# A decoder layer on one core: reciprocal denominators written widened by VectorE, the first group's projections in idle banks, and the last two attention rows in two lanes

## The chip, the core and the metric

The kernel runs on one core of one Trainium2 chip. A core has five engines, each with a queue of its own that it works off in order: TensorE (PE; its weight loads are shown apart, as PEld), VectorE (DVE), ScalarE (ACT), GpSimd (POOL) and SyncE (SP), which here only issues DMAs. Engines wait for each other through semaphores. The metric is the device time of one execution in microseconds (us).

## What is computed

64 rows of 128 tokens by 512 features pass through one decoder layer of three parts, each with a layer norm ahead and a residual add behind:

```python
x = x + mixer(layernorm(x))                 # state space mixer
x = x + cross_attention(layernorm(x), ctx)  # banded attention, 8 heads
x = x + experts(layernorm(x))               # top 2 of 8 experts

# mixer
h_in, gate = split(x @ in_proj_w.T)                  # 1024 channels each
u  = silu(causal_conv4(h_in) + conv_b)
ts, Bm, Cm = split(u @ x_proj_w.T)                   # 128, 16, 16
dt = softplus(ts @ dt_proj_w.T + dt_proj_b)
h  = scan(exp(dt * A), dt * u * Bm)                  # 16 states for each channel
y  = ((h * Cm).sum(states) + D * u) * silu(gate)
return y @ out_proj_w.T

# attention of one row (the 512 features are the sequence, the 128 tokens the embedding)
attn = softmax(q @ k.T / 4 within a band of 64)      # 8 heads of 16
o = (attn @ v) @ w_out.T + b_out
return w_ct.T @ (relu(o.T) * ctx) + b_ct
```

## The kernel before

The 64 rows are taken in 32 groups of two (`GB = 2`, `NG = 32`, so `NT = 256` columns). The work is a software pipeline over groups, written out by hand. `iteration(g, cur, nxt, p1, p2)` stands once in each engine's block. It runs the 64 scan steps of group `g` (`cur`), the preparation of group `g + 1` (`nxt`: layer norm, input projections, convolution, `ts`, B and C rows, step sizes), the output projection and attention of group `g - 1` (`p1`), and the experts of group `g - 2` (`p2`). The order on each engine is the order of the lines in `iteration`: there is no scheduler at run time. Iteration -1 only prepares group 0, iterations 1 to 31 have scans and attention both, iteration 32 has only the attention of the last group and the experts of the one before, iteration 33 only the last experts.

The scan of one step takes one decay tile that ScalarE writes into one of two PSUM banks (`decays`), one product that GpSimd writes into a ring of eight SBUF slots (`times_b`), and VectorE's scan instruction (`scan`). The result is multiplied by C, 40 times on GpSimd and 24 times on VectorE (`times_c`), and TensorE sums it over states by transposes into bank 2 (`y_sum`).

PSUM has eight banks: 0 and 1 for decays, 2 for `y_sum`, 3 (`PS_B`) for every projection of the preparation, 4 to 7 (`PS_ATT`) for attention, experts and the output projection.

In the preparation each projection of group `j` goes through the one bank `PS_B`. `h_in(j, q)` makes 256 channels of `h_in`. `tap3` (ScalarE) and six instructions of `conv` (VectorE) read it from the bank, so the next `h_in` or `gate_in` waits for `conv_done`. `gate_raw` copies a gate projection out. `ts_in`, `bc_in_rows` and four `dt_in` follow through the same bank. The weights `w_in` come in eight pieces through two SBUF slots; SyncE issues a piece when the projection that used its slot is done.

Attention of row `b` of a group goes, per row: `proj` (q and k), `v`, four pairs of scores `s` and row maximum `max`, `shift` and `addq`, four `st` (transposed scores) with eight `exp`, two `av` with two copies `o`, then `den` (TensorE transposes the outputs, which carry the softmax sums in every 32nd column), `rden`, `rep`, `on`, `wo`, `enc`, `ct` and `x2`. Rows share one set of tiles (`qk`, `probs`, `xb`, `v_aug`, `nmax`, `o_sb`, `enc`) and the banks 4 to 7, so the two rows of a group follow each other. Around the denominators VectorE takes 32 reciprocals per partition out of PSUM, ScalarE repeats each 32 times, and TensorE transposes the 1024 columns back (`rep`, which waits for `rden_wide`):

```python
nc.vector.reciprocal(rden[:].rearrange("p (j a) -> p j a", j=NJ), ps[:, PS_ATT + 2:PS_ATT + 4, DH:512:32])
nc.scalar.copy(rden_rep.rearrange("p (a r) -> p a r", r=32),
               rden[:].rearrange("p (a r) -> p a r", r=1).to_broadcast([P, NBLK * NHEAD, 32]))
```

Of the kernel before, what the change touches and what calls it, by code (L numbers as in the profile page):

```python
# [5 lines left out]
def decoder_layer(nc, x_d, ctx_d, w_in_d, conv_w_d, conv_b_d, w_xt_d, w_xbc_d, w_dt_d, dt_b_d, a_log_d,  # L6
# [9 lines left out]
    P = 128  # L16
    B, T, H = x_d.shape
    GB = 2
# [29 lines left out]
    with stack:  # L48
# [57 lines left out]
        rden = sb("rden", [P, NBLK * NHEAD])  # L106
# [12 lines left out]
        def part(mem, at, *dims):  # L119
# [45 lines left out]
        den_ps, rden_done, rden_wide, rrep_ps, on_done, wo_ps, enc_used, ct_ps, x2_done = [  # L165
            sem(k) for k in ("den_ps", "rden_done", "rden_wide", "rrep_ps", "on_done", "wo_ps", "enc_used", "ct_ps", "x2_done")]
# [45 lines left out]

        @block.sync
        def _(sp):
# [18 lines left out]
            def context(i):  # L233
                reached(sp, ln_aggr["e"], i)
                sp.dma_start(enc[:], ctx_d[i]).then_inc(enc_in, 16)

            def iteration(g, cur, nxt, p1, p2):
# [6 lines left out]
                if p1:  # L244
                    context((g - 1) * GB)
# [18 lines left out]
                if p1:  # L264
                    context((g - 1) * GB + 1)
# [29 lines left out]
        def _(pool):  # L295
# [36 lines left out]

            def iteration(g, cur, nxt, p1, p2):
                if p1:
                    times_c(g - 1, 62)
                if cur:
                    times_b(g, 0)
                    times_b(g, 1)
                    times_b(g, 2)
                if p2:  # L340
                    rstd("e", g - 2, 0, 2)
                if cur:
                    times_b(g, 3)
# [5 lines left out]
                    times_b(g, 6)  # L349
                    times_b(g, 7)  # L350
                    times_b(g, 8)
                    times_c(g, 5)
                    times_b(g, 9)
                    times_c(g, 6)
                    times_b(g, 10)
                if nxt:
                    rstd("a", g + 1, 0, 2)
                if cur:
                    times_b(g, 11)
                if p1:  # L360
                    rstd("t", g - 1, 0)
                if cur:
                    times_c(g, 8)
                    times_b(g, 12)
                    times_b(g, 13)
                    times_b(g, 14)
                    times_c(g, 10)
                    times_b(g, 15)
                    times_b(g, 16)
                    times_c(g, 11)  # L370
# [3 lines left out]
                    times_b(g, 19)  # L374
                    times_c(g, 14)
                if p1:
                    rstd("t", g - 1, 1)
                if cur:
                    times_b(g, 20)
                    times_c(g, 16)  # L380
                    times_b(g, 21)
                    times_c(g, 18)
                    times_b(g, 22)
                    times_c(g, 19)
# [1568 lines left out]
```

## Time and profile before

| | us |
|---|---|
| median of 3 runs | 4977.84 (4977.36 to 4978.13) |
| the profiled execution, whole | 4972.81 |
| its span in the trace | 4971.0 |
| TensorE busy | 4574.1 (92%) |
| VectorE busy | 4434.0 (89%) |
| ScalarE busy | 4400.9 (89%) |
| GpSimd busy | 4196.7 (84%) |

The span is what the trace covers; 1.8 us of the profiled execution lie around it. The profile page gives the busy time of each engine, the chain of work that ended last, and the costliest groups of instructions; the trace behind it answers by stage, by line and by wait. Most of the span is the same iteration repeated, so one stretch of one period stands for it, and the opening and the end are read apart.

### The profile page before, as it was taken

The numbers are of one execution on the slowest core, as the hardware profiler recorded it, in microseconds if no ns is written. First come the engines' busy times: TensorE is split into PE (matmuls) and PEld (weight loads), VectorE is DVE, ScalarE is ACT, GpSimd is POOL, SyncE is SP. The second block draws the span as 40 slices with busy tenths as digits, with TensorE's granted clock in tenths as the row PEclk, the third lists the DMA queues.
The fourth block names the chain that finished last, engine by engine and source line by source line (L and its number), as shares of the span: only waits on it lengthen the run. The fifth ranks groups of instructions, "written<-read, shape, count | busy, mean of one in ns | idle before, by whom it ended". The sixth has DMA issues, their size and how long they took to land.

```text
span 4971.0 us, 143017 instructions
## 1 busy us (share of the span) xinstructions
PE 4574.1 (92%) x52548; PEld 3357.0 (68%) x52548; DVE 4434.0 (89%) x6051; ACT 4400.9 (89%) x9310; POOL 4196.7 (84%) x3467
## 2 busy tenths in 40 slices
PE   4799999999999999999999999999999999999976
PEld 3666666766766776776776767676666677666653
DVE  2899999999999999999999999999999999999961
ACT  3798999999999999999999999999999999999862
POOL 2988898888898888898888898888889888888860
PEclk8899999999999999999999999999999999999996
DMA  3212222212222221222221222221222221122100
GB/s 124 79 46 71 76 78 78 82 54 67 76 78 78 82 69 52 82 76 78 78 82 38 85 77 75 81 82 40 80 76 78 78 82 56 64 77 77 65 14 7
DMA packets 119316, 350.46 MB, mean 71 GB/s; under 512 B 18688, under 2 KB 19456, under 8 KB 118528
## 3 DMA queue, kind: packets, MB, share of 16 engines
q1 hardware_dynamic: 118656, 341.51, 20.7%
q8 instruction: 432, 7.08, 0.6%
q14 instruction: 228, 1.87, 0.1%
HBM read 323.64 MB, written 17.83 MB: 69 GB/s over the span
## 4 chain that ended last, share of the span: by engine, by line
PE 47%; DVE 18%; POOL 12%; issue 11%; ACT 8%; DMA 2%; DVEq 1%; SPq 0%; ACTq 0%; POOLq 0%
PE ps L1204 9%; PE ps L1156 9%; POOL ring L320 8%; PE ps L1224 5%; DVE ring L1542 5%; POOL ring L329 4%; DVE ps L1542 4%; PE ps L1100 4%; PE ps L1111 3%; DVE nmax L1564 3%; ACT ps L498 3%; PE ps L1072 3%; PE ps L1233 2%; DMA x_new<-in_x 2%; PE ps L1034 1%
## 5 line engine op out<-in xcount | busy, mean ns | idle before, releaser
L320 POOL TENSOR_TENSOR ring<-du,bc 128x512 f32<-128x512 f32 x2048 | 2579.3, 1277 | 486.6 <-PE ps L1156 368.0
L498 ACT ACTIVATE ps<-delta,a_neg 128x254 f32<-128x254 f32 x4096 | 1771.6, 468 | 39.5 <-DVE ring L1542 31.3
L329 POOL TENSOR_TENSOR ring<-ring,bc 128x512 f32<-128x512 f32 x1280 | 1621.6, 1277 | 110.7 <-DVE ring L1542 109.5
L1542 DVE TENSOR_TENSOR_SCAN ring<-ps,ring 128x512 f32<-128x512 f32 x1280 | 1542.5, 1213 | 143.9 <-ACT ps L498 123.9
L1156 PE MATMUL ps<-ident,ring 128*128 128x128 f32 x8192 | 1073.3, 276 | 70.2 <-POOL ring L329 65.5
L1156 PEld LDWEIGHTS ps<-ident,ring 128*128 128x128 f32 x8192 | 925.0, 142 | 179.1 <-issue 99.6
L1542 DVE TENSOR_TENSOR_SCAN ps<-ps,ring 128x512 f32<-128x512 f32 x768 | 933.5, 1215 | 48.8 <-ACT ps L498 39.2
L1526 DVE TENSOR_TENSOR ring<-ps,bc 128x512 f32<-128x512 f32 x768 | 526.4, 685 | 19.0
L657 ACT ACTIVATE probs_mem<-ps 128x768 f32<-128x768 f32 (+1 forms) x512 | 449.8, 912 | 66.8 <-PE ps L1100 63.4
L1224 PE MATMUL ps<-w_in,xt_a 128*128 128x256 f32 x2048 | 484.2, 391 | 20.9 <-ACT delta L550 12.0
L1204 PE MATMUL ps<-xt_a,w_in 128*128 128x256 f32 x2048 | 475.9, 386 | 8.5 <-DVE hc L1646 4.1
L1224 PEld LDWEIGHTS ps<-w_in,xt_a 128*128 128x128 f32 x2048 | 390.2, 194 | 123.8 <-issue 43.0
L1186 PE MATMUL ps<-w_outp,yz 128*128 128x512 f32 x1024 | 465.6, 598 | 8.5 <-ACT yz L591 4.9
L1204 PEld LDWEIGHTS ps<-xt_a,w_in 128*128 128x128 f32 x2048 | 381.5, 191 | 73.7 <-issue 9.9
L1646 DVE SCALAR_TENSOR_TENSOR hc<-ps,conv_w,hc 128x254 f32<-128x254 f32 (+2 forms) x768 | 359.8, 476 | 58.1 <-ACT hc L602 39.9
L1564 DVE TENSOR_REDUCE nmax<-ps 128x8 f32<-128x1280 f32 x256 | 377.7, 1475 | 32.0 <-PE ps L1072 32.0
L1186 PEld LDWEIGHTS ps<-w_outp,yz 128*128 128x128 f32 x1024 | 187.5, 191 | 202.1 <-issue 188.2
L1072 PE MATMUL ps<-qk 32*32 32x160 f32 (+2 forms) x16384 | 296.1, 297 | 0.0
L1100 PE MATMUL ps<-qk 32*128 32x192 f32 (+1 forms) x4096 | 271.9, 380 | 0.0
L1047 PE MATMUL ps<-xb,w_qk 128*128 128x512 f32 x512 | 251.4, 604 | 2.5 <-ACT ps L518 1.1
L1111 PE MATMUL ps<-probs_mem,v_aug 128*32 128x192 f32 (+1 forms) x4096 | 227.8, 364 | 18.6 <-ACT probs_mem L657 18.6
L498 ACT ACT_TABLE_LOAD x187 | 239.9, 1283 | 3.3
(140 smaller groups left out, 6381.0 us busy)
## 6 DMA issues: line engine op xcount, KB each, us to landing
w_in<-in_w_in SPq DMA_DIRECT2D x256, 512.0 KB, 3.6
bc<-bc_rows SPq DMA_DIRECT2D x256, 512.0 KB, 5.5
x_new<-in_x SPq DMA_DIRECT2D x32, 512.0 KB, 6.7
x_res<-in_x SPq DMA_DIRECT2D x32, 512.0 KB, 6.2
enc<-in_ctx SPq DMA_DIRECT2D x64, 256.0 KB, 3.2
out<-x_att SPq DMA_DIRECT2D x32, 512.0 KB, 3.2
w_outp<-in_w_outp SPq DMA_DIRECT2D x1, 2048.0 KB, 7.9
bc_rows<-bc_sb SPq DMA_DIRECT2D x128, 8.0 KB, 1.5
```

The source lines that it names most:

```text
L320: nc.gpsimd.tensor_tensor(ring[:, s % RING, :].rearrange("p (n t) -> p n t", n=2), du[:, q % 2, (ic % 2) * NT:(ic % 2 + 1) * NT].rearrange ...
L329: nc.gpsimd.tensor_tensor(ring[:, s % RING, :], ring[:, s % RING, :], bc[:, s % RS, 2:4, :].rearrange("p a t -> p (a t)"), ALU.mult).then_ ...
L498: nc.scalar.activation(ps[:, bank("step", s), (n % 2) * NT:(n % 2 + 1) * NT].rearrange("p (b t) -> p b t", b=GB)[:, :, 1:T], delta[:, ic, ...
L657: nc.scalar.activation(probs[:, :, blk, lo:hi], ps[:, PS_ATT:PS_ATT + 4, (n % 2) * WIN + lo:(n % 2) * WIN + hi], ACT.Exp).then_inc(p_done, 1)
L1100: last = nc.tensor.matmul(ps[:, PS_ATT + hp, a * WIN + lo:a * WIN + hi], qk[r:r + 32, 2 + j, blk * P:(blk + 1) * P], qk[r:r + 32, j, at:at ...
L1156: last = nc.tensor.matmul(ps[:, PS_Y, b * T:(b + 1) * T], ring[:, t % RING, n * NT + b * T:n * NT + (b + 1) * T], ident[:], start=False, s ...
L1186: last = nc.tensor.matmul(ps[:, PS_ATT + b, :], yz[:, ic, b * T:(b + 1) * T], w_outp[:, ic, :], start=(ic == 0), stop=(ic == NI - 1))
L1204: last = nc.tensor.matmul(ps[:, PS_B, a * NT:(a + 1) * NT], w_in[:, slot, k, a * P:(a + 1) * P], xt_a[:, k, :], start=(k == 0), stop=(k == ...
L1224: last = nc.tensor.matmul(ps[:, PS_B, b * NT:(b + 1) * NT], xt_a[:, k, b * T:(b + 1) * T], w_in[:, slot, k, :], start=(k == 0), stop=(k == ...
L1526: nc.vector.tensor_tensor(ring[:, s % RING, :], ps[:, bank("step", s), :], bc[:, s % RS, 2:4, :].rearrange("p a t -> p (a t)"), ALU.mult). ...
L1542: nc.vector.tensor_tensor_scan(state, ps[:, bank("step", s), :], ring[:, s % RING, :], 0.0, ALU.mult, ALU.add).then_inc(h_done, 1)
L1564: nc.vector.tensor_reduce(nmax[:, n].rearrange("p j (a r) -> p a j r", r=32)[:, :, :, DH], ps[:, PS_ATT:PS_ATT + 4, 0:NJ * NEAR].rearrange ...
```

## The change

Four things change, in one new version.

**Denominators.** `rden` and the semaphore `rden_wide` are gone. VectorE's reciprocal now reads a view of the 32 PSUM columns that repeats each 32 times and writes the 1024 columns of `rden_rep` itself; ScalarE's copy is gone; TensorE's `rep` waits for `rden_done`.

**First group.** `prep_bank(j, use, q)` gives for group 0 (`first(j)`) the banks 4 to 7 to the four `h_in`, 4 to `ts`, 5 to the B and C rows, and 6, 7, 4 to the first three `dt_in`; gates stay in `PS_B`. Their waits for the shared bank go. The order of iteration -1 is written as `first_iteration`: the third gate projection moves ahead of `ts_in`, the first `dt_in` ahead of `bc_in_rows`, and `soft_one` ahead of `soft_ln`.

**Last group.** A second set of tiles, semaphores and banks (0 to 3), a `Lane`, is laid over tiles that are idle once the last scans are over (`hc0`, `bc`, `xt_a`). In iteration 32 row 1 uses it, and the order of that iteration, `last_iteration`, interleaves the two rows. GpSimd clears the new `v_aug` and `nmax` there (`second_lane`).

**Order.** The lines of `iteration` stand in another order on all engines but SyncE; no instruction is added to or taken from the repeated iteration but for the denominators.

```diff
+        def prep_bank(j, use, q=0):
+
+            if not first(j):
+                return PS_B
+            return {"h": PS_ATT + q, "ts": PS_ATT, "bc": PS_ATT + 1, "dt": (PS_ATT + 2, PS_ATT + 3, PS_ATT, PS_B)[q]}[use]
...
+        def lane(g, b):
+
+            return lanes[1 if isinstance(g, int) and g == NG and b == 1 else 0]
...
-                else:
-
-                    act.wait_ge(rden_done, i + 1)
-                    nc.scalar.copy(rden_rep.rearrange("p (a r) -> p a r", r=32),
-                                   rden[:].rearrange("p (a r) -> p a r", r=1).to_broadcast([P, NBLK * NHEAD, 32])).then_inc(rden_wide, 1)
...
-                    pe.wait_ge(rden_wide, i + 1)
+                    pe.wait_ge(L.rden_done, i + 1)
...
-                if q < 2:
+                if first(j):
+                    pass
+                elif q < 2:
...
-                        last = nc.tensor.matmul(ps[:, PS_B, a * NT:(a + 1) * NT], w_in[:, slot, k, a * P:(a + 1) * P],
+                        last = nc.tensor.matmul(ps[:, prep_bank(j, "h", q), a * NT:(a + 1) * NT], w_in[:, slot, k, a * P:(a + 1) * P],
...
-                    dve.wait_ge(den_ps, i + 1)
-                    nc.vector.reciprocal(rden[:].rearrange("p (j a) -> p j a", j=NJ), ps[:, PS_ATT + 2:PS_ATT + 4, DH:512:32]).then_inc(rden_done, 1)
+                    dve.wait_ge(L.den_ps, i + 1)
+                    nc.vector.reciprocal(
+                        L.rden_rep.rearrange("p (j a r) -> p j a r", j=NJ, r=32),
+                        ps[:, L.bank + 2:L.bank + 4, DH:512:32].rearrange("p j (a r) -> p j a r", r=1)
+                        .to_broadcast([P, NJ, NBLK * NHEAD // NJ, 32])).then_inc(L.rden_done, 1)
```

In the order that follows, scans are printed as SCALAR_TENSOR_TENSOR on `ps` or `ring`. On VectorE, at the denominators of row 1 in a repeated iteration, before:

```order
L1542 SCALAR_TENSOR_TENSOR ps<-ps,ring 128x512
L1574 RECIPROCAL rden<-ps 128x32
L1525 REGISTER_ALU
L1526 TENSOR_TENSOR ring<-ps,bc 128x512
L1539 ISA
L1542 SCALAR_TENSOR_TENSOR ring<-ps,ring 128x512
L1532 REGISTER_ALU
L1535 TENSOR_TENSOR yg<-ps,gate_t 128x256
L1578 TENSOR_TENSOR o_sb<-ps,o_sb 128x512 x2
```

At the same place in the changed kernel:

```order
L1773 SCALAR_TENSOR_TENSOR ring<-ps,ring 128x512
L1807 RECIPROCAL probs_mem<-ps 128x1024
L1770 REGISTER_ALU
L1773 SCALAR_TENSOR_TENSOR ring<-ps,ring 128x512
L1814 TENSOR_TENSOR o_sb<-ps,o_sb 128x512 x2
```

The reciprocal writes 1024 columns in place of 32, and one instruction, a scan, stands between it and the use of its result in place of three.

On TensorE, in the last iteration with scans, from `den` of row 1 to `rep` and `wo`, before:

```order
L1121 MATMUL ps<-ident,o_sb 128x128 x8
L1156 MATMUL ps<-ident,ring 128x128 x16
L1130 MATMUL ps<-ident,probs_mem 128x128 x8
L1149 MATMUL ps<-ident,skip 128x128 x2
L1156 MATMUL ps<-ident,ring 128x128 x8
L1136 MATMUL ps<-o_sb,w_o 128x512 x2
```

And in the changed kernel:

```order
L1272 MATMUL ps<-ident,o_sb 128x128 x8
L1307 MATMUL ps<-ident,ring 128x128 x8
L1281 MATMUL ps<-ident,probs_mem 128x128 x8
L1287 MATMUL ps<-o_sb,w_o 128x512 x2
```

Less stands between the transposes that feed the reciprocals and those that take them up.

On TensorE at the very end of attention, in iteration 32, the changed kernel has, from `den` of row 0 on (tiles `hc` and `bc` are row 1's):

```order
L1272 MATMUL ps<-ident,o_sb 128x128 x8
L1262 MATMUL ps<-bc 32x192 x4
L1262 MATMUL ps<-bc 32x256 x8
L1262 MATMUL ps<-bc 32x192 x4
L1281 MATMUL ps<-ident,probs_mem 128x128 x8
L1183 MATMUL ps<-band,ident_bf 32x512 x16
L1251 MATMUL ps<-hc 128x192 x4
L1251 MATMUL ps<-hc 128x256 x4
L1287 MATMUL ps<-o_sb,w_o 128x512 x2
```

Before, nothing of row 1 but two projections stood between row 0's denominators and its end.

## Rows read from the trace of the kernel before

**Rows 1.** The page: span, and busy time of each engine.
```profile
span 4971.0 us, 143017 instructions
PE 4574.1 (92%) x52548; PEld 3357.0 (68%) x52548; DVE 4434.0 (89%) x6051; ACT 4400.9 (89%) x9310; POOL 4196.7 (84%) x3467
```

**Rows 2.** Windows, two periods: stretch, length, busy PE, PEld, DVE, ACT, POOL, clock, DMA.
```profile
1169.00:1316.60 147.60, 140.58 (x1643) 103.60 (x1643) 138.27 (x190) 137.15 (x292) 130.97 (x108) 1.00 0.22 73
1316.60:1464.20 147.60, 140.58 (x1644) 103.72 (x1643) 138.43 (x190) 137.41 (x292) 131.10 (x109) 1.00 0.23 73
```

**Rows 3.** Waits in 1169 to 1316.6: who waited for whom, us, times, longest.
```profile
DVE ring L1542 <- ACT ps L498: 3.4, 3, 2.2
PE ps L1018 <- DVE nmax L1564: 3.3, 4, 1.2
...
DVE ps L1542 <- ACT ps L498: 1.2, 1, 1.2
...
DVE rden L1574 <- PE ps L1121: 0.9, 2, 0.6
```

**Rows 4.** Groups by line, whole span: shapes, count, busy, mean ns, idle before.
```profile
L1526 DVE TENSOR_TENSOR ring<-ps,bc 128x512 f32<-128x512 f32 x768 | 526.4, 685 | 19.0
...
L1535 DVE TENSOR_TENSOR yg<-ps,gate_t 128x256 f32<-128x256 f32 x256 | 105.7, 413 | 21.5 <-PE ps L1156 21.5
...
L665 ACT COPY probs_mem<-rden 128x1024 f32<-128x1024 f32 x64 | 66.7, 1043 | 9.6 <-DVE rden L1574 9.6
...
L1574 DVE RECIPROCAL rden<-ps 128x32 f32<-128x32 f32 x64 | 22.8, 357 | 83.0 <-PE ps L1121 83.0
...
L1493 DVE COPY held<-neg_half 128x1 f32<-128x1 f32 x64 | 9.8, 153 | 2.2
...
L1615 DVE RECIPROCAL small<-small 128x2 f32<-128x2 f32 x32 | 5.3, 166 | 1.1
```

**Rows 5.** Chain that ended last, opening: start, length, engine and line.
```profile
29.16 5.14 PE ps L1204 x16
34.30 0.02 issue
34.32 1.03 ACT hc L602 x2
...
38.36 5.42 PE ps L1204 x16
...
53.92 3.73 PE ps L1204 x16
...
71.56 1.03 ACT hc L602 x2
...
76.25 5.42 PE ps L1233 x16
81.69 0.38 ACT ts L626
...
101.63 0.81 ACT ps L498 x2
```

**Rows 6.** DMA issues in 0 to 100 us: KB each, median us to landing.
```profile
w_in<-in_w_in SPq DMA_DIRECT2D x9, 512.0 KB, 3.6
```

**Rows 7.** Timeline, opening: start, length, instruction, idle before it and releaser.
```profile
91.82 1.28 ACT L577 ACT_TABLE_LOAD   x1
...
96.89 0.69 DVE L1521 TENSOR_TENSOR du<-ps,u 128x512 f32<-128x512 f32 x1
```

**Rows 8.** Windows of the end: row 0's attention, row 1's, last experts (columns as rows 2).
```profile
4836.00:4894.00 58.00, 38.69 (x538) 21.20 (x537) 10.56 (x13) 17.37 (x23) 0.54 (x1) 0.68 0.03 10
4894.00:4947.00 53.00, 32.41 (x518) 17.87 (x516) 11.15 (x14) 10.72 (x16) 0.00 (x0) 0.68 0.02 6
```

**Rows 9.** Timeline of PE in row 0's attention (columns as rows 7).
```profile
4844.59 0.31 PE L1018 MATMUL ps<-band,ident 32*128 32x320 bf16 x4 [1.59 <-DVE nmax L1564]
...
4868.50 3.21 PE L1111 MATMUL ps<-probs_mem,v_aug 128*32 128x192 f32 x32 [1.84 <-ACT probs_mem L657]
...
4886.80 1.09 PE L1130 MATMUL ps<-ident,probs_mem 128*128 128x128 f32 x8 [1.53 <-ACT probs_mem L665]
```

More of the change, by code:

```diff
@@ L2 @@
 from concourse import mybir
+from collections import namedtuple
 from contextlib import ExitStack
@@ L1210, in gate_in @@
                 slot, k = ((1, 1), (1, 2), (1, 3), (0, 3))[q]
-                if q < 2:
+                if first(j) and q < 3:
+                    pe.wait_ge(xt_done["a"], 2)
+                    reached(pe, gate_done, q)
+                elif q < 2:
                     if cur:
@@ L1245, in dt_in @@
             def dt_in(j, q, cur):
-                if q == 0:
+                if first(j) and q < 3:
+                    pass
+                elif q == 0:
                     if cur:
@@ L1296, in iteration @@
                 if cur:
+                    y_sum(g, 1)
                     y_sum(g, 3)
@@ L1407, in iteration @@
                 if p1:
-                    attention(g, p2, 1, "shift")
+                    attention(g, p2, 1, "s", 3)
                 if cur:
@@ L1411, in iteration @@
                 if p1:
+                    attention(g, p2, 1, "shift")
+                if cur:
+                    y_sum(g, 43)
+                if p1:
                     attention(g, p2, 1, "st", 0)
                 if cur:
-                    y_sum(g, 43)
                     y_sum(g, 45)
@@ L1682, in iteration @@
                 if cur:
-                    scan(g, 8)
-                    scan(g, 9)
-                    times_c(g, 9)
+                    scan(g, 11)
+                if p2:
+                    router(g - 2, 1)
+                if cur:
+                    scan(g, 12)
+                if p2:
+                    experts_gated(g - 2)
+                if p1:
+                    shift("t", g - 1, 0)
+                    mixer_add(g - 1, 1)
+                if cur:
+                    times_c(g, 12)
+                    y_step(g, 0)
+                if p2:
+                    experts_add(g - 2, 0)
+                if cur:
+                    scan(g, 13)
+                    scan(g, 14)
+                    scan(g, 15)
                 if nxt:
@@ L1788, in iteration @@
                     conv(j, 4)
+                if cur:
+                    soft_step(4, g, 3)
                 if p1:
-                    attention(g, 0, "enc")
+                    attention(g, 0, "on")
                 if nxt:
@@ L1793, in iteration @@
                 if cur:
+                    y_step(g, 3)
                     scan(g, 37)
                 if p1:
-                    attention(g, 0, "x2")
+                    attention(g, 0, "enc")
                 if cur:
```

951 lines of the change are left out of this document (595 added, 356 removed).

## Prediction, made before the changed kernel was run

> **What bounds the kernel now.** I read the page's busy times first [rows 1]: four engines at 84 to 92% of the span, so no share alone says who sets the time. Then two windows one period apart [rows 2]. A period is 147.6 us, the second window repeats the first within 0.3 us of busy time on every engine, and PE is busy for 140.6 of it, DVE for 138.3 to 138.4, ACT for 137.2 to 137.4, POOL for 131. PE has 7.0 us left, DVE 9.25, ACT 10.3. The reader should see that whatever adds more than 9.25 us to DVE in a period must lengthen the period, whatever the order. The waits of one period [rows 3] tell what this slack is: DVE waits 4.6 us for decays from ACT and 0.9 us for the denominators' transposes, PE waits 3.3 us for row maxima. The engines hold each other in a chain with small gaps everywhere. 31 iterations (1 to 31) have scans and attention both, so each us of a period is 31 us of the run. Opening and end stand apart: before the first scan [rows 5] and from 4836 us on [rows 8] one chain runs and the engines are mostly idle.
>
> **Denominators, the term that decides.** Removed: ACT's copy of 1024 columns, 1043 ns, 64 times [rows 4]. Replaced: DVE's reciprocal of 32 columns, 357 ns, by one of 1024 columns. Its price is in no row, so I bound it from both sides. A plain DVE instruction reading PSUM takes 685 ns for 512 columns and 413 for 256 [rows 4], 1.06 ns a column and 141 ns fixed. By that rate 32 columns would be 175 ns. The reciprocal takes 357, 182 more. Either each column of a reciprocal is dearer, or reading columns that lie 32 apart is (5.7 ns for each of the 32). The two differ by a factor of five here, because the new form computes 1024 reciprocals and visits only 32 places.
>
> The other reciprocal in the trace decides as far as anything does: 128x2, out of SBUF and not apart, takes 166 ns against 153 for a copy of one column [rows 4]. A plain second column would add 1 ns, it is 13. From 2 to 32 columns the two reciprocals rise by 191 ns, 6.37 ns a column, and that line leads back to 153 ns at none, the fixed time of the copy. One rate explains both rows. So I take 6.37 ns: 357 + 992 x 6.37 = 6.68 us. The lower end is 141 + 1024 x 1.06 + 32 x 5.7 = 1.41 us; a gain against 357 ns is excluded, since the form writes 32 times the columns. The upper end is 357/32 = 11.2 ns a column, 11.4 us, far since the fixed part is then counted 32 times.
>
> The Trainium skill, VectorE: DVE Perf Modes, section "Walkthrough: the 8-slice pipeline in each mode", says that a reciprocal runs an iterative divide with a repeat count of 8 where a simple operation gives a result each cycle. The trace agrees that it is dearer (6.37 against 1.06 ns), though as six times, not eight. What eight would make of the sum is a rival below.
>
> In a period: two rows, 2 x (6.68 - 0.36) = 12.6 us more on DVE, 138.35 + 12.6 = 151.0 busy, already 3.4 over today's period. ACT gets 2.1 us less, worth nothing while DVE is the bound. How much of DVE's 9.25 us idle stays? Its own wait for `den` (0.9) can go. Behind the reciprocal queue the scans: ACT has only two decay banks, so it fills them and stops for some 4 us each time, and so does POOL when its slots are full; PE waits at `rep` with `y_sum` behind it. These engines then have to make up other work, and some of the 4.6 us of waits for decays comes back. I keep 5.2 us, a little over half. The ends are none kept (151.0) and all kept (160.2). Period 151.0 + 5.2 = 156.2, 8.6 more, times 31: **+267**. The ends are +105 and +392.
>
> **Order.** PE has less to do between `den` and `rep`, and one scan stands before `on` on DVE where three instructions stood. This suits a short reciprocal: with 6.7 us PE stands at `rep`. I give the new order nothing for itself, within 1 us a period either way; its other moves shift single steps among neighbours and add no instruction.
>
> **First group.** In the chain `h_in` 0 ends at 34.3; `tap3` and `conv` follow and PE resumes at 38.36; so before each of two `h_in`/gate steps some 4.1 us go [rows 5]. With own banks PE goes on at once. What is late next is the weights: a piece is issued when its slot is free and lands in 3.6 us [rows 6], about as long as a projection (3.73 us where PE came to it without a long pause, 5.42 after one [rows 5]). The slots alternate, so landing hides behind the other slot's work. Seven projections from 29.2 at 3.7 to 5.4 each bring `h_in` 3 to its end by 56.5 to 61.3, then tap, conv, `u` (71.56 to 76.25 takes 4.7 us) give `ts_in` at 61 to 67 against 76.25: 9 to 15, take 12. Behind it `soft_one` ahead of `soft_ln` lets two of the four DVE steps, 0.7 us each, run during the table load and logarithm, and one step size less stands before the exponential: 4 us before `du` (96.89 [rows 7]). The rest of the opening (POOL, decays at 101.63) follows `du`. Sum **-16**, ends -12 and -20. What hides here costs nothing later: the third gate projection runs in time that PE waits anyway.
>
> **Last group.** Rows 0 and 1 take 58 and 53 us, PE busy for 38.7 and 32.4 of them, so 39.9 us idle [rows 8], in gaps of 1.6 us behind each maximum, 1.8 behind exponentials, 1.5 before `rep` [rows 9]. Each row's gaps can take the other's work. Not coverable: row 1's own last stretch (4.5 us of gaps) and some 3 us where both rows wait for ACT: gain 32. The long reciprocal takes back part: row 0's `rep` has one `av` of 3.21 us [rows 9] ahead of it against 6.7 us, 3.5 of wait in place of 1.5, and row 1's stands alone, 6.7 in place of 0.36 + 1.04. That is 7.3: **-25**, ends -15 and -35. The memsets and the new `enc` load are done long before row 1 needs them.
>
> **Sum.** +267 - 16 - 25 = +226. On the profiled execution, 4972.8 (span 4971.0 and 1.8 around it), 5199. The median shown is 5.0 above that execution: **5204 us**.
>
> **Rivals.**
> - *The reciprocal is cheap and the distance of the columns was dear (faster).* Price 1.41 us. DVE gets 2.1 us a period more, 140.5 of 147.6, ACT 2.1 less; the period stays. Sum -16 - 32 = -48: 4930, or 4899 to 4961 with the order's 1 us a period. For it: no other DVE instruction in the trace reads PSUM columns apart, so that rate is not refuted; 13 ns on a 128x2 instruction is little to stand on. Against: it needs a second reason for those 13 ns. It decides below about (9.25 - some 5)/2 + 0.36, say 2.5 us an instruction. The Trainium skill, Advanced Engine Details and Errata, section "Memory Cachelines", gives PSUM lines of two FP32 values and says that accesses which aren't contiguous slow matmuls; no run here shows it for VectorE, and it speaks for this rival.
> - *DVE's slack takes all it can.* Period 151.0, +105 - 41: 5042. Against it speaks that waits for decays exist at 94% load already.
> - *Nothing is absorbed.* The chain takes the whole 12.6 us: +392 - 41: 5329.
> - *Eight plain columns' time for each reciprocal.* 8 x 1.06 = 8.5 ns, fixed 86 from the 357: 8.8 us. DVE 155.2 busy, + 5.2 kept: period 160.4, +397 - 16 - 21: 5338. Against: the 128x2 row would need 149 fixed and the 128x32 row 86. The page of the skill named above is this rule.
> - *The edit on the first group does nothing* because the weights come late: 12 us less gain, inside every case.
>
> **Chances.** Forecast (5100 to 5270) 46%; slack takes all (below 5100) 9%; nothing absorbed or eightfold (above 5270) 15%; cheap reciprocal 29%; a cheap one with an order that loses as much again, about no change, 1%. The likeliest case alone would span 5035 to 5335. Both signs hold much, so the range reaches over: 4905 to 5300 leaves out some 4% below and 10% above. A measurement of this kernel can tell about 0.2%, 10 us. Faster by more 28%, within 1%, slower by more 71%.
>
> **What would show it.** The row of the reciprocal 128x1024 on DVE: 6.7 us by the forecast, 1.4 by the first rival, 8.8 by the eightfold; this one number decides most. Then the period: 156 with DVE at 151 busy, against 147.6 with DVE at 140.5. PE should wait at `rep` by some us a row. The first scan should start some 16 us earlier (near 86), and the last maximum of row 1 should fall among row 0's exponentials, with 80 to 86 us from the first q/k projection to row 1's end in place of 111. I am wrong if the rate was the distance's, or if engines that stop during the reciprocal cannot catch up.

## The result, and the profile after

| kernel | median of 4 runs, us | lowest to highest | profiled execution, us |
|---|---|---|---|
| before | 4977.6 | 4977.1 to 4978.1 | 4972.8 |
| changed | 5331.3 | 5325.7 to 5336.6 | 5329.3 |

The changed kernel takes 1.071 times as long (95% interval 1.069 to 1.073): slower, as forecast, but by 354 us where 226 had been forecast, and 31 us above the range's upper end of 5300.

The page of the changed kernel, span and busy times, answers [rows 1]:

```profile
span 5327.4 us, 142925 instructions
...
PE 4705.1 (88%) x52548; PEld 3408.5 (64%) x52548; DVE 4796.5 (90%) x6051; ACT 4355.7 (82%) x9216; POOL 4198.0 (79%) x3470
```

DVE has 362 us more work, ACT 45 less, and PE, whose list of matmuls is the same 52548, is busy 131 us longer. The last is the first hint of something that the forecast did not have.

Two periods of the changed kernel in the view of windows (columns as [rows 2]):

```profile
1075.20:1236.00 160.80, 144.67 (x1642) 105.04 (x1642) 149.62 (x190) 135.98 (x289) 131.07 (x109) 0.98 0.20 67
1236.00:1397.00 161.00, 144.95 (x1632) 104.29 (x1632) 148.26 (x189) 134.69 (x286) 130.00 (x108) 0.97 0.20 67
```

Against [rows 2] the period went from 147.6 to 160.8 and 161.0. DVE's busy time is 148.3 to 149.6, near the forecast's 151.0. But it is idle for 11.2 and 12.7 us, where it was for 9.25 before: it has more work *and* more idle time. PE is busy 4.2 us longer and idle for 16 in place of 7.0, and its granted clock is no longer 1.00. Measured from ScalarE's copy of `ts` for group 2 to the one for group 31, 29 periods, the mean period went from 148.1 to 161.2. All later periods in this text are this mean. The windows over these 29 periods, the kernel before and then the changed one:

```profile
354.73:4649.77 4295.04, 4081.59 (x47622) 3008.26 (x47623) 4014.18 (x5482) 3984.32 (x8441) 3802.66 (x3133) 1.00 0.22 73
```
```profile
342.31:5016.78 4674.47, 4220.25 (x47623) 3061.31 (x47619) 4340.66 (x5482) 3944.95 (x8353) 3802.35 (x3133) 0.97 0.20 67
```

Divided by 29, DVE's busy time went from 138.4 to 149.7 us a period and its idle time from 9.7 to 11.5. PE's busy time went from 140.7 to 145.5.

The groups of the changed kernel by line (columns as [rows 4]):

```profile
L350 POOL TENSOR_TENSOR ring<-du,bc 128x512 f32<-128x512 f32 x2048 | 2573.8, 1278 | 689.5 <-PE ps L1307 520.4 <-DVE du L1752 167.5
L555 ACT ACTIVATE ps<-delta,a_neg 128x254 f32<-128x254 f32 x4096 | 1765.8, 468 | 189.1 <-DVE ring L1773 184.9
L359 POOL TENSOR_TENSOR ring<-ring,bc 128x512 f32<-128x512 f32 x1280 | 1625.7, 1279 | 293.7 <-DVE ring L1773 292.4 <-issue 0.7
...
L1807 DVE RECIPROCAL probs_mem<-ps 128x1024 f32<-128x1024 f32 x63 | 412.0, 6540 | 8.9 <-PE ps L1272 8.8
...
L1281 PE MATMUL ps<-ident,probs_mem 128*128 128x128 f32 x504 | 105.9, 379 | 246.1 <-DVE probs_mem L1807 246.1
```

The reciprocal takes 6.54 us; the forecast said 6.68. PE stands 246 us in all at `rep` (L1281). The other engines stand too: ACT at its decays for 189 us, POOL for 689.5 and 293.7. In the kernel before these rows read:

```profile
L320 POOL TENSOR_TENSOR ring<-du,bc 128x512 f32<-128x512 f32 x2048 | 2579.3, 1277 | 486.6 <-PE ps L1156 368.0 <-DVE du L1521 116.8 <-issue 0.7
L498 ACT ACTIVATE ps<-delta,a_neg 128x254 f32<-128x254 f32 x4096 | 1771.6, 468 | 39.5 <-DVE ring L1542 31.3
L329 POOL TENSOR_TENSOR ring<-ring,bc 128x512 f32<-128x512 f32 x1280 | 1621.6, 1277 | 110.7 <-DVE ring L1542 109.5 <-issue 1.2
...
L1130 PE MATMUL ps<-ident,probs_mem 128*128 128x128 f32 x512 | 66.5, 273 | 3.7 <-ACT probs_mem L665 3.7
```

The `rep` matmul itself went from 273 to 379 ns. It comes right after a stop of PE, at a lower clock. Windows of 20 us around the reciprocal that starts at 1318.28, in the changed kernel:

```profile
1296.00:1316.00 20.00, 18.19 (x278) 12.66 (x262) 14.35 (x17) 17.43 (x37) 17.08 (x15) 0.91 0.02 4
1316.00:1336.00 20.00, 15.02 (x78) 11.44 (x71) 16.99 (x15) 12.49 (x25) 10.92 (x9) 0.83 0.46 157
```

The granted clock has two levels, full speed (2.4 GHz) and half (1.2 GHz); 0.91 and 0.83 are means over the stretch. In the second stretch PE stood for 4.98 us at `rep` until 1324.87. In windows of 10 us the clock is 1.00 from 1310 to 1320 and 0.70 from 1320 to 1330. The 0.91 of the first stretch is an earlier fall: 0.83 from 1300 to 1310, behind a stretch of 10 us in which PE, with several short waits, was busy for 6.91. [rows 2] have a mean of 1.00.

The waits of the period from 1075.2 to 1236.0 (columns as [rows 3]):

```profile
POOL ring L350 <- PE ps L1307: 16.7, 7, 8.2
POOL ring L359 <- DVE ring L1773: 10.1, 7, 3.8
...
PE ps L1281 <- DVE probs_mem L1807: 7.7, 2, 5.0
ACT ps L555 <- DVE ring L1773: 5.6, 9, 2.9
DVE ps L1773 <- ACT ps L555: 4.8, 3, 3.8
```

Against [rows 3]: DVE's wait for decays from ACT, 4.6 us in a period before, is 4.8 in this line alone. In this period it did not shrink to make room.

The opening, timeline of PE (columns as [rows 7]):

```profile
28.90 9.55 PE L1357 MATMUL ps<-xt_a,w_in 128*128 128x256 f32 x32 [0.77 <-ACT xt_a L653]
38.70 3.69 PE L1380 MATMUL ps<-w_in,xt_a 128*128 128x256 f32 x16 [0.25 <-DMA w_in<-in_w_in]
42.23 3.62 PE L1357 MATMUL ps<-xt_a,w_in 128*128 128x256 f32 x16
...
58.00 3.72 PE L1389 MATMUL ps<-u,w_xt 128*128 128x256 f32 x16 [0.81 <-ACT u L667]
```

PE runs through all seven projections (the first row holds two of them) with gaps of about 0.25 us for a piece of weights. `ts_in` starts at 58.00, 76.25 before [rows 5]. The first scan starts at 77.31, before at 101.58: 24.3 us gained.

The end, from the first q/k projection to the end of row 1's cross-attention, in the view of windows: first the kernel before, then the changed one (columns as [rows 2]):

```profile
4836.10:4946.96 110.86, 71.00 (x1053) 38.96 (x1051) 21.71 (x26) 28.07 (x38) 0.54 (x1) 0.68 0.02 8
```
```profile
5220.60:5303.30 82.70, 59.83 (x1059) 33.89 (x1058) 37.31 (x44) 27.25 (x39) 0.00 (x0) 0.88 0.04 11
```

110.9 us became 82.7. The two long reciprocals lie bare in the chain that ended last (start, length, what):

```profile
5267.16 6.57 DVE probs_mem L1807
...
5287.32 6.57 DVE bc L1807
```

**The account.** From the start of the first scan to the start of the last one the kernels take 4712.0 and 5123.8 us: +411.8 over 32 iterations, 31 of them with attention. Opening: -24.3. From there to the end 157.4 and 126.3: -31.1. Together +356, the difference of the spans.

### The profile page after: what moved, and what is told of

The parts are those of the page before. It is cut to its first block, busy times and chain, and to the rows that moved or that the text cites. A ratio compares the mean times of both kernels' runs of the same rounds, so it can differ in the third digit from the quotient of the medians.

```text
span 5327.4 us, 142925 instructions
## 1 busy us (share of the span) xinstructions
PE 4705.1 (88%) x52548; PEld 3408.5 (64%) x52548; DVE 4796.5 (90%) x6051; ACT 4355.7 (82%) x9216; POOL 4198.0 (79%) x3470
## 4 chain that ended last, share of the span: by engine, by line
PE 59%; DVE 20%; issue 14%; ACT 3%; POOL 2%; DVEq 1%; ACTq 0%; POOLq 0%
PE ps L1307 10%; PE ps L1380 8%; PE ps L1337 8%; PE ps L1357 4%; DVE probs_mem L1807 4%; PE ps L1251 4%; PE ps L1262 3%; DVE ring L1773 3%; PE ps L1223 3%; DVE ps L1773 3%; PE ps L1196 2%; DVE hc L1882 2%; PE ps L1389 2%; DVE nmax L1797 2%; PE ps L1183 2%
## 5 line engine op out<-in xcount | busy, mean ns | idle before, releaser
L350 POOL TENSOR_TENSOR ring<-du,bc 128x512 f32<-128x512 f32 x2048 | 2573.8, 1278 | 689.5 <-PE ps L1307 520.4
L359 POOL TENSOR_TENSOR ring<-ring,bc 128x512 f32<-128x512 f32 x1280 | 1625.7, 1279 | 293.7 <-DVE ring L1773 292.4
L1773 DVE TENSOR_TENSOR_SCAN ring<-ps,ring 128x512 f32<-128x512 f32 x1280 | 1535.1, 1210 | 53.3 <-ACT ps L555 50.3
L1757 DVE TENSOR_TENSOR ring<-ps,bc 128x512 f32<-128x512 f32 x768 | 525.7, 685 | 12.4
L717 ACT ACTIVATE probs_mem<-ps 128x768 f32<-128x768 f32 x504 | 444.6, 915 | 88.9 <-PE ps L1251 88.4
L1380 PE MATMUL ps<-w_in,xt_a 128*128 128x256 f32 x2048 | 472.0, 384 | 14.8 <-ACT delta L608 13.1
L1807 DVE RECIPROCAL probs_mem<-ps 128x1024 f32<-128x1024 f32 x63 | 412.0, 6540 | 8.9 <-PE ps L1272 8.8
L1281 PE MATMUL ps<-ident,probs_mem 128*128 128x128 f32 x504 | 105.9, 379 | 246.1 <-DVE probs_mem L1807 246.1
L704 ACT ACTIVATE qk<-ps,b_qk 128x512 f32<-128x512 f32 x252 | 171.0, 678 | 166.9 <-PE ps L1196 166.8
L1251 PE MATMUL ps<-qk 32*128 32x192 f32 x4032 | 263.4, 375 | 0.0
```

The source lines that it names most:

```text
L350: nc.gpsimd.tensor_tensor(ring[:, s % RING, :].rearrange("p (n t) -> p n t", n=2), du[:, q % 2, (ic % 2) * NT:(ic % 2 + 1) * NT].rearrange ...
L359: nc.gpsimd.tensor_tensor(ring[:, s % RING, :], ring[:, s % RING, :], bc[:, s % RS, 2:4, :].rearrange("p a t -> p (a t)"), ALU.mult).then_ ...
L1251: last = nc.tensor.matmul(ps[:, L.bank + hp, a * WIN + lo:a * WIN + hi], L.qk[r:r + 32, 2 + j, blk * P:(blk + 1) * P], L.qk[r:r + 32, j, a ...
L1380: last = nc.tensor.matmul(ps[:, PS_B, b * NT:(b + 1) * NT], xt_a[:, k, b * T:(b + 1) * T], w_in[:, slot, k, :], start=(k == 0), stop=(k == ...
L1757: nc.vector.tensor_tensor(ring[:, s % RING, :], ps[:, bank("step", s), :], bc[:, s % RS, 2:4, :].rearrange("p a t -> p (a t)"), ALU.mult). ...
L1773: nc.vector.tensor_tensor_scan(state, ps[:, bank("step", s), :], ring[:, s % RING, :], 0.0, ALU.mult, ALU.add).then_inc(h_done, 1)
```

## The experiments

Each kernel was timed in three rounds beside the kernel before, which gave four times of each and ten of e7; only e6, the one with reciprocals of near columns, ran once. "Order before" and "order after" are the two lists of steps of the repeated iteration.

| kernel | order | denominators | median, us | ratio to before (95%) | period, us |
|---|---|---|---|---|---|
| e1_two_step | after | as before | 5015.9 | 1.007 (1.006 to 1.009) | 151.6 |
| e2_wide_only | before | widened | 5429.3 | 1.090 (1.089 to 1.092) | 162.4 |
| e3_wide_copy | after | widened, plain copy | 4926.2 | 0.990 (0.988 to 0.991) | 148.75 |
| e4_halves | after | widened, in halves | 5360.7 | 1.077 (1.075 to 1.079) | 162.3 |
| e5_rep_later | after, `rep` later | widened | 5515.8 | 1.107 (1.106 to 1.109) | 167.4 |
| e6_near_columns | after | as before, other columns | 5016.8 | one run | 151.6 |
| e7_dve_copy | after | 32, then DVE's copy | 4994.4 | 1.003 (1.002 to 1.004) | 150.6 |
| e8_first_only | before | as before | 4955.2 | 0.996 (0.994 to 0.998) | 148.2 |
| e9_last_only | before | as before | 4930.4 | 0.992 (0.990 to 0.993) | 148.2 |
| e10_old_order | before | as before | 4909.4 | 0.986 (0.984 to 0.987) | 148.15 |
| e11_old_order_wide_copy | before | widened, plain copy | 4935.6 | 0.992 (0.990 to 0.993) | 149.0 |
| e12_unwaited | before | as before, and idle work | 5477.8 | 1.101 (1.099 to 1.103) | 164.0 |

e1, e3 to e7, e10 and e11 have the new opening and end; e2 and e12 have neither; e8 and e9 have one each.

### Whose time is the reciprocal's: the divide's or the distance's

e3 takes the changed kernel and puts a plain copy of the same view in place of the divide (the reciprocal is left out):

```diff
-                    nc.vector.reciprocal(
+                    nc.vector.tensor_copy(
                         L.rden_rep.rearrange("p (j a r) -> p j a r", j=NJ, r=32),
```

> The changed kernel with the widened reciprocal replaced by a plain copy of the same view (the reciprocal itself is left out, so outputs are scaled by the sums). Theory rate (the reciprocal's 6.2 ns a column is the divide's): the instruction takes 1.2 to 1.4 us, the period 147 to 148, 4920 us. Theory distance (reading columns 32 apart is what costs): the copy takes about 6.5 us as well if each repeated read pays again, 1.4 us if only the 32 places pay; at 1.23 us the distance costs nothing. Time at 6.5 us: 5331 us.

e6 goes back to 32 reciprocals and ACT's copy, but reads 16 columns side by side in each bank in place of columns 32 apart (so the denominators are other numbers). e1 is the same with the right columns, and the edit is shown against it:

```diff
-                                         ps[:, L.bank + 2:L.bank + 4, DH:512:32]).then_inc(L.rden_done, 1)
+                                         ps[:, L.bank + 2:L.bank + 4, 0:NBLK * NHEAD // NJ]).then_inc(L.rden_done, 1)
```

> As e1 (32 reciprocals, ScalarE's copy, new order), but the reciprocals read 16 columns side by side in each of the two banks, not 32 apart; the denominators are then the wrong ones. Theory rate: the 128x32 reciprocal stays at 340 to 357 ns. Theory distance: it falls to some 175 ns. The run's time is that of e1, 5016 us.

The instruction's group by line, in e3, in e6 and in e1:

```profile
L1807 DVE COPY probs_mem<-ps 128x1024 f32<-128x1024 f32 x63 | 76.1, 1207 | 8.1 <-PE ps L1272 8.0
```
```profile
L1820 DVE RECIPROCAL rden<-ps 128x32 f32<-128x32 f32 x63 | 21.5, 341 | 9.0 <-PE ps L1285 9.0
```
```profile
L1820 DVE RECIPROCAL rden<-ps 128x32 f32<-128x32 f32 x63 | 21.4, 340 | 8.1 <-PE ps L1285 8.1
```

The copy that visits the same columns takes 1.21 us. The plain rate gives 1.23 (141 ns + 1024 x 1.06), and the first rival's 1.41 charged the distance on top. Reciprocals of near and far columns take 341 and 340 ns. The distance costs nothing here and the divide costs all: (6540 - 340) / 992 = 6.25 ns a column, forecast 6.37. The kernel follows: with a cheap wide instruction it beats the one before, and 5.33 us more in each of 64 instructions cost 405 us.

### Where DVE's idle time went

e2 puts the widened reciprocal alone into the kernel before: ACT's "wide" steps go, PE's wait before `rep` is for `rden_done`, the order stays.

```diff
-                    nc.vector.reciprocal(rden[:].rearrange("p (j a) -> p j a", j=NJ), ps[:, PS_ATT + 2:PS_ATT + 4, DH:512:32]).then_inc(rden_done, 1)
+                    nc.vector.reciprocal(
+                        rden_rep.rearrange("p (j a r) -> p j a r", j=NJ, r=32),
...
-                if p1:
-                    attention(g, p2, 0, "wide")
```

> The kernel before with the widened reciprocal alone (ScalarE's copy gone); order, opening and end of before. Theory A (each microsecond of the block goes into the period in either order): 31 x 13.4 = 415 and some 10 for the last two rows, 4977.6 + 425 = 5400 us, period 161. Theory B (the new order, which has little between den and rep, makes part of it): period 156, some 5250 us, DVE idle 5 us a period.

The period rose by 14.3 us for 12.4 more on DVE, 1.16 us for each, although ACT had 2.1 us less to do. DVE is busy 150.2 of 162.4, so 12.2 idle: in the old order too the idle time grew. That is more than the rival "nothing is absorbed" charged.

Two readings were left. Either somebody stands for the result (PE at `rep`, with `y_sum` queued behind it), or a stop of DVE costs its time whoever waits for the result. e12 tells them apart: the kernel before, and behind each row's 32 reciprocals a maximum over 6144 columns that nobody reads.

```diff
+                    reached(dve, idle_done, i)
+                    nc.vector.tensor_reduce(idle_out[:], w_dt[:].rearrange("p (r k) -> p r k", r=1).to_broadcast([P, 6, 1024]),
+                                            AX.X, ALU.max).then_inc(idle_done, 1)
```

> The kernel before, complete, with one more VectorE instruction behind each row's 32 reciprocals: a maximum over 6144 columns of a constant into six columns that nobody reads. It takes about 6.5 us and no engine waits for it directly; TensorE's rep gets its denominators before it begins. Theory time (a stop of VectorE of this length costs its whole length whoever waits for it, since the scans, decay banks and ring behind it stop): period 161 to 164, 5380 to 5460 us, near e2's 5429. Theory stand (most of e2's loss is TensorE standing at rep for the result): the period is 152 to 156, 5100 to 5230 us.

The timeline of e12 around one of these, rows of all engines with long lengths or waits:

```profile
1196.64 6.49 DVE L1578 TENSOR_REDUCE idle_out<-w_dt 128x6 f32<-128x6144 f32 x1
...
1197.04 1.03 PE L1259 MATMUL ps<-ts,w_dt 128*128 128x256 f32 x4
...
1203.76 0.17 ACT L497 COPY ps<-zeros 128x4 f32<-128x4 f32 x1 [5.96 <-DVE ring L1528]
...
1204.93 1.27 POOL L331 TENSOR_TENSOR ring<-ring,bc 128x512 f32<-128x512 f32 x1 [5.57 <-DVE ring L1544]
...
1205.54 2.07 PE L1259 MATMUL ps<-ts,w_dt 128*128 128x256 f32 x4 [5.72 <-ACT delta L552]
```

And its windows, one period and then the 10 us from 1200:

```profile
1150.00:1314.00 164.00, 145.80 (x1644) 106.43 (x1643) 151.03 (x192) 138.19 (x291) 131.16 (x108) 0.96 0.20 66
```
```profile
1200.00:1210.00 10.00, 4.46 (x15) 3.86 (x16) 9.31 (x9) 6.03 (x13) 3.70 (x3) 0.71 0.49 161
```

Nobody waits for the maximum itself, and the period still rises by 15.9 us for 13.0 of DVE, more than in e2. This is the mechanism, read downward: DVE stops scanning for 6.5 us. ACT has filled its two decay banks, makes its one copy and stands 5.96. POOL stands 5.57 for a slot that a scan must free. PE stands 5.72, not for DVE at all but for a step size (`delta`) that stands behind the decays in ACT's list. All four engines have stopped. Then PE's same four matmuls of L1259 take 2.07 us in place of 1.03, since the clock has fallen to half. The other maximum of the period stops them later: ACT stands 6.37 us and POOL 3.23 behind it, and PE, which had a projection and `rep` to run first, stands at the end for `on`, a step of DVE that came late behind the maximum:

```profile
1309.64 1.22 PE L1138 MATMUL ps<-o_sb,w_o 128*128 128x512 f32 x1 [5.48 <-DVE o_sb L1583]
```

So e12 shows that nobody need wait for the result; it does not show the loss without a stand of PE, which it has twice a period. None of DVE's 9.25 us of idle was used up. I read this so: the idle time lies in small waits elsewhere in the period, and nothing is stored up across the stop. PE is also busy longer, 145.8 against 140.6 in [rows 2], at the lower clock.

Would smaller blocks help? e4 makes each reciprocal two of 512 columns, with scans between them (the second behind scan 36 in row 0's case, behind scan 59 in row 1's), and PE waits for each half apart:

```diff
-                    attention(g, 0, "rden")
+                    attention(g, 0, "rden", 0)
...
+                if p1:
+                    attention(g, 0, "rden", 1)
```

> The changed kernel with the widened reciprocal cut into two of 512 columns, with soft_step 2 and scan 36 between them for row 0 and scan 59 for row 1; TensorE takes each half up on its own. VectorE's load grows by 0.1 us at most. Theory block (a stop of 6.5 us outlasts the two decay banks and the ring, and TensorE stands at rep): the period falls from 161.1 to 154 to 157, 5110 to 5200 us. Theory load (it is VectorE's sum of work whatever its pieces): the period stays at 160 to 161, 5320 to 5340 us.

Each half takes 3.34 us, and the period is 162.3, 1.1 longer than the changed kernel's. Two short stops cost as much as one long one, and a little more. That a stop under some length is free, as the two banks of decays might suggest, did not show at 3.3 us. But only a scan, or a scan and one short step, stood between the halves; halves further apart were not tried.

e5 moves PE's `rep` and `wo` some steps later, past `y_sum` 33 and `y_sum` 57, and DVE's `on` behind `y_step` 3 and 6, so that PE need not stand with `y_sum` behind it:

```diff
-                    attention(g, p2, 0, "rep")
...
+                    y_sum(g, 33)
+                if p1:
+                    attention(g, p2, 0, "rep")
```

> The changed kernel with the widened reciprocal, and TensorE's rep of each row moved behind work that does not need it (row 0: behind both projections of row 1; row 1: behind dt 2 and y_sum 57), VectorE's on moved behind y_step. Theory stand (TensorE standing at rep, 7.7 us a period, and the lower clock behind it are what keeps the slack from being used): the period falls from 161.2 to 152 to 156, 5050 to 5170 us. Theory reach (the late scans themselves hold ScalarE's banks, GpSimd's ring and conv, wherever rep stands): the period stays at 158 to 162, 5230 to 5360 us, and TensorE waits elsewhere.

It is the slowest of all, period 167.4. In its waits of one period PE's stand is not gone but moved:

```profile
PE ps L1300 <- DVE yg L1767: 11.3, 2, 5.8
...
DVE o_sb L1815 <- PE ps L1281: 6.9, 3, 3.4
```

PE stands 5.5 and 5.8 us for `yg`, the step that DVE makes after the reciprocal, and DVE now waits for `rep`. This move was a poor one and shows only that the stand at `rep` cannot be dodged by a few steps.

### The order

e1 is the changed kernel with the two-step denominators put back, ACT's copy behind `soft_one(g, 3)` and `step_size(j, 0)`. e10 is e1 with the order before. So the order alone differs between them.

```diff
+                if p1:
+                    attention(g, p2, 0, "wide")
```

> The changed kernel with the denominators as before: VectorE takes 32 reciprocals, ScalarE repeats them 32 times (its copy stands behind soft_one 3 and behind step size 0 in the repeated iteration). Opening, last group and order stay. Theory A (the reciprocal's 6.54 us is the whole loss, and opening and end keep their gains): the period falls from 161.1 to 147.6, the opening stays 24.3 us shorter and the end 28 to 33 us shorter, so 4977.6 - 55 = 4922 us. Theory B (the new order is part of the loss): the period stays above 149, more than 4965 us.

> The order of the repeated iteration as before and ScalarE's copy as before, with the changed opening and the two lanes at the end. Theory order (the new order, not the denominators, is why e1 lost): the period is 148.1 as before, the opening 24 us and the end 28 to 33 us shorter: 4980 - 55 = 4925 us. Theory sum (opening and end gain less when the rest is as before, because time saved is waited for in the first or last full iteration): 4940 to 4970 us.

With the short form the new order costs 3.5 us a period (151.6 against 148.15), 107 us in all. In e1's waits DVE stands 10.3 us for decays where it stood 4.6 [rows 3]:

```profile
DVE ps L1786 <- ACT ps L557: 6.4, 4, 2.9
...
DVE ring L1786 <- ACT ps L557: 3.9, 4, 2.0
```

The copy of 1.04 us stands ahead of decays in ACT's list, and e3, which has the new order without it, has a period of 148.75. That the copy's place makes the decays late is argued from this; another place was not tried.

e11 is e10 with the wide plain copy (the reciprocal is left out), to be set against e3:

```diff
-                    nc.vector.reciprocal(
+                    nc.vector.tensor_copy(
```

> As e10 (order of before, opening and end changed), with VectorE's plain copy of the view (1.21 us) in place of 32 reciprocals and ScalarE's copy; the reciprocal is left out. Against e3 (4926, new order, same instruction) it tells the order apart: theory order-made-for-it (the new order suits the widened form): 4930 to 4950 us, slower than e3. Theory old-order-better: the period is 148 or less, at or below e10's 4909 us.

With the wide form the orders come within 0.2 us a period (149.0 old, 148.75 new). With the widened reciprocal the new one is 1.2 us better (161.2 against e2's 162.4). So the new order is made for the widened form and gains a little there; for the old form it is a loss. No run with it has a shorter period than the 148.1 of the kernel before. The wide plain copy on DVE is not better than ACT's copy either: e11 is 26 us slower than e10, though ACT has 2.1 us less to do in a period. This pair also shows what a short piece costs: two instructions of 1.23 us in place of two of 0.36 put 1.7 us on DVE, and the period rose by 0.8. Half of it was absorbed, with less work on ACT at the same time; of the long reciprocals nothing was.

### Opening and end alone

e8 has only the new opening, e9 only the two rows side by side at the end, both on the old order and denominators. In e8:

```diff
-            return lanes[1 if isinstance(g, int) and g == NG and b == 1 else 0]
+            return lanes[0]
```

> Order of the repeated iteration, denominators and last group as before; only the first group's projections in idle banks with their order. First scan at 77 to 78 us in place of 101.6, period 148.1: 4978 - 24 = 4954 us. Rival (iteration 0 waits for what it now meets too early, DMA rows or weights): half of the gain, 4966.

> Order of the repeated iteration, denominators and opening as before; only the last group's two rows in two lanes. By e10, where both together gave 68 us and the opening 24, the end gives 44: 4978 - 44 = 4934 us. By the working of the forecast, 32: 4946 us.

In medians e8 gains 20 us and e9 45. The end of e10, again from the first q/k projection to row 1's end:

```profile
4815.40:4883.80 68.40, 53.00 (x1060) 30.50 (x1059) 24.88 (x44) 30.31 (x43) 0.00 (x0) 1.00 0.04 14
```

110.9 us before, 82.7 in the changed kernel, 68.4 here. The same matmuls keep PE busy for 71.0, 59.8 and 53.0 us, at a granted clock of 0.68, 0.88 and 1.00. That was not in the sum: with the gaps of one row filled by the other's work the clock stays up, and PE's shorter busy time is 18 of the 42.5 us; the other 24.5 are gaps filled (39.9 us idle before, 15.4 here). The two long reciprocals take back 14.3 us (82.7 - 68.4): PE is idle 7.5 us longer (22.9) and busy 6.8 us longer, at the lower clock.

### VectorE does both steps

e7 keeps 32 reciprocals and lets DVE widen them out of SBUF, 1024 columns:

```diff
+                    dve.wait_ge(rden_narrow[k], i + 1)
+                    nc.vector.tensor_copy(L.rden_rep.rearrange("p (a r) -> p a r", r=32),
```

> The changed kernel with VectorE taking 32 reciprocals into a small tile and then repeating them itself by a copy out of SBUF. If only the count of divides was dear, VectorE has 0.36 and at most 1.21 us (the plain copy of e3) in place of 6.54 and the period is 148 to 150, 4920 to 4960 us, with a right output. If out of SBUF the copy of repeated columns runs at a better rate, 0.6 us, it is at e3's 4926 or 5 us below. Rival (two dependent instructions on VectorE cost a round of semaphores each): 0.2 us more a row, 10 us on top.

The group of the copy, and DVE and POOL around one of them (timeline):

```profile
L1813 DVE COPY probs_mem<-rden 128x1024 f32<-128x1024 f32 x63 | 137.6, 2184 | 2.2
```
```profile
4863.63 5.27 DVE L1813 COPY probs_mem<-rden 128x1024 f32<-128x1024 f32 x1
...
4868.83 1.21 DVE L1775 TENSOR_TENSOR_SCAN ring<-ps,ring 128x512 f32<-128x512 f32 x1
```
```profile
4863.44 2.48 POOL L361 TENSOR_TENSOR ring<-ring,bc 128x512 f32<-128x512 f32 x2
4865.88 2.47 POOL L352 TENSOR_TENSOR ring<-du,bc 128x512 f32<-128x512 f32 x2
```

The copy takes 694 ns where POOL is idle, in the last iteration. Beside POOL it takes from 1.6 to 6.08 us. In each of the 62 copies beside POOL its end lies 0.55 us behind the end of one of POOL's instructions (here 4865.88 + 2.47 = 4868.35, and 4863.63 + 5.27 = 4868.90): it gets its turn only when one of POOL's is over, and here four of them in a row went ahead of it. The other way round POOL waits too: in 30 of the 62 cases the copy got in between two of POOL's instructions that follow each other at once, and the second took 1.72 to 1.73 us, where no other in this kernel or in e10 took more than 1.33:

```profile
1252.93 1.27 POOL L361 TENSOR_TENSOR ring<-ring,bc 128x512 f32<-128x512 f32 x1 [0.28 <-DVE ring L1775]
1254.16 1.72 POOL L352 TENSOR_TENSOR ring<-du,bc 128x512 f32<-128x512 f32 x1
```

That copy ran from 1253.13 to 1254.75. It began 0.03 us behind the end of the reciprocals that it needs (1252.77 + 0.33), so the rival's 0.2 us for two dependent instructions did not show. e7's period is 150.6, 1.0 below e1's with the same order and 2.4 above e10's with the order before.

### The best version

e10, the kernel before with the new opening and end only, runs in 4909.4 us (4908.3 to 4910.2), ratio 0.986 (0.984 to 0.987): 1.4% faster than the kernel before, and 7.9% less time than the changed one.

## Why the prediction was right or wrong

- **Direction, and the term that decides it: right.** The price of the reciprocal was forecast at 6.68 us and is 6.54. The argument from the small 128x2 row held; e3 and e6 show that the rate is the divide's. The rival of the cheap reciprocal (29%) is refuted by both. The eightfold one is refuted by the same row (8.8 us forecast, 6.54 measured). The Trainium skill, VectorE: DVE Perf Modes, section "Walkthrough: the 8-slice pipeline in each mode", gives the divide a repeat count of 8 and no time. The trace agrees that it is dear, but at 6.25 ns a column, six times the 1.06 of a plain column and not eight. What the Trainium skill, Advanced Engine Details and Errata, section "Memory Cachelines", says of matmuls, and what spoke for the distance, does not carry over to VectorE here: 341 against 340 ns.
- **The step that failed: "How much of DVE's 9.25 us idle stays? I keep 5.2".** It kept 5.2; the windows after show 11.2 and 12.7. The period grew by 13.1 us (148.1 to 161.2), not by 8.6, and the stretch with scans by 411.8 us, not 267: 145 us too little. Opening and end gave back 14 of that (-55.4 in place of -41), which leaves the miss of 128. I had named the reason for keeping idle time (two decay banks, full slots, `y_sum` behind `rep`) and then took a value in the middle, as if idle time were a store that other work can be moved into. e12 shows that for stops of this length it is not: 13.0 us whose result nobody waits for cost 15.9. DVE's mean idle time grew, from 9.7 to 11.5, in place of shrinking to 5.2.
- **The upper end was too low.** The stated range ended at 5300, under my own rival of 5329, and the term's end, +392, stood at "nothing is absorbed", 1.00 us of period for each on DVE. The changed kernel against the one before has 1.06 (13.1 for 12.4, with a copy less on ACT and another order). Three other comparisons lie higher: 1.16 (e2), 1.17 (e3 to the changed kernel, 12.4 us of period for 10.7 of DVE) and 1.22 (e12). In all of them PE is busy longer at a lower granted clock: 145.5 (changed kernel), 145.9 (e2) and 145.8 us (e12) a period, against 140.7 before and 141.9 in e3. A mean clock of 0.97 over a period of 161 us is some 4 to 5 us of full speed lost (an estimate from these windows), so the clock accounts for PE's longer work; that it makes the whole excess is not shown. [rows 2] show a clock of 1.00 and [rows 8] 0.68 where PE has gaps; the rows for this term were there and I did not join them.
- **"Nothing is absorbed: 5329" looks exact against 5331.3 and is so only in part.** It had +392 for the periods, which came out at +412, and -41 for opening and end, which came out at -55.4. The two errors, +20 and -14, nearly cancel.
- **Order, ±1 us a period: about right for the form that the change has** (e3, e11: 0.2 better; changed against e2: 1.2 better, a little outside). For the old form it would have been wrong, by 3.5.
- **Opening, -16 with ends -12 and -20: too small, -24.3.** The mechanism was right (PE goes on at once, a piece of weights lands just in time), its sizes were not. `ts_in` came 18.3 us earlier, not 12, and the part behind it gave 6.0, not 4. I took 3.7 to 5.4 us for a projection; the first took 6.1 and the other six 3.6 to 3.7. I also made `h_in` 3 the seventh of the seven, and it is the sixth: the trace has it done at 53.3, and the third gate runs while `u` is made. The 56.5 and 61.3 of the working do not follow from its numbers either: seven times 3.7 and 5.4 from 29.2 end at 55.1 and 67.0. In the median of e8 the gain is 20.
- **End, -25 with ends -15 and -35: inside, -31.1, by errors that partly cancel.** Without the long reciprocals I had a gain of 32; e9 and e10 gain 45 and 46. In e10's window the filled gaps are 24.5 us, less than 32, and 18 come from PE's work at the full clock, which I had put at nothing. What the long reciprocals take back was forecast at 7.3 us of waits. PE's idle time grows by 7.5, as forecast; the other 6.8 of the 14.3 are the clock again.
- **Chances.** I gave 15% to all times above 5270. Two of my own reasons spoke for more: at 94% load there were waits already, and the buffers between the engines hold 2 banks, some 4 us of work.

What stays open: how what the period gained beyond DVE's own added time splits between the lower clock and the stops themselves in the changed kernel. A kernel with the stop but without the fall of the clock wasn't tried, nor one with halves of the reciprocal far apart.

## What to carry to other kernels

When four engines hand work to one another through a few buffers, a long instruction on one stops the others before it is over (in e12's row 1 after 1.2 to 3.2 us of its 6.5). So count its whole length into the period and don't subtract idle time that lies in small gaps; then look at whether TensorE's stand lowers its clock. A short addition can be absorbed in part (e11: 1.7 us cost 0.8). Before widening an operation to save a copy, price a divide by the columns that it writes, from the smallest such row in the trace. Where one chain runs alone, side-by-side work can pay twice, for the gap and for the clock (e10: 24.5 and 18 us).

## What the runs showed of the hardware that was not expected

- A reciprocal on VectorE costs 6.25 ns for each column that it writes: 340 ns for 32, 3335 for 512 (e4), 6540 for 1024. Columns 32 apart or side by side made no difference. A plain copy of the same 1024 broadcast columns out of PSUM takes 1207 ns in all (1197 to 1225).
- The SBUF-to-SBUF copy on VectorE and GpSimd's instructions took turns by whole instructions: 694 ns alone, 2.2 us on average and up to 6079 ns beside GpSimd, whose own next instruction took 1.73 us in place of 1.28 in 30 cases. The Trainium skill, SBUF — State Buffer, section "🔬 SBUF: two separate sides", says that GpSimd and a VectorE instruction in a mode of two ports share a pair of ports, which the one that starts first locks for its whole length. The trace agrees, and shows more: the copy got in between two of GpSimd's back-to-back instructions in 30 cases and was passed over in others, by four and five in a row in the two longest.
- The maximum over 6144 columns out of SBUF took 6494 to 6498 ns in all 64 cases, 62 of them beside the same GpSimd work, so not every read of SBUF is held up.
- In e12 TensorE's granted clock fell to half (1.2 GHz) for a part of the 10 us in which it stood for more than 5 (0.71 as a mean), and the matmuls behind the stop took twice their time (2.07 against 1.03 us).
